# One-hot tables of the edge-MLP pass: four comparisons with a scalar per partition in place of one with two broadcast inputs

## The chip, the core and the metric

The kernel runs on one core of one Trainium2 chip. The metric is the device time of one execution in microseconds (us). Engines are named as in the profile: PE is TensorE, PEld its weight loads, DVE is VectorE, ACT is ScalarE, POOL is GpSimd, SP is SyncE. "TensorE clock" is the clock that the throttle granted, as a share of full speed.

## The reference

A graph network of four layers over 3125 nodes of 128 features and 100,000 edges that are sorted by destination. Each layer adds its result to the residual stream. The layer that this case touches is the second, a message pass with an MLP on every edge:

```
h = relu(layernorm(x))
x1   = concat(h[src], h[dst], edge_attr)          # 128 + 128 + 64 features
msgs = gelu(gelu(x1 @ mW1 + mb1) @ mW2 + mb2) @ mW3 + mb3
agg  = segment_sum(msgs, dst) / count
u    = gelu(concat(h, agg) @ uW1 + ub1) @ uW2 + ub2
x    = x + layernorm(u + h) * gamma + beta
```

The other layers are a GAT of three rounds (first), a GATv2 of two rounds with four heads (third), and a GCN of two rounds (fourth).

## The kernel before, in words

The edges are sorted into blocks of 128 destination nodes (25 blocks) and padded, so that a group of 512 edges has destinations in one block only. There are `NG` = 220 groups; a group is 4 tiles of 128 edges (`TG` = 4), with one edge per partition and the tile number along the free axis. `c.dlo[p, g, q]` holds, as an fp32 number, the destination of the edge at partition p, tile q, group g, counted from its block's first node. `c.iota` is a row 0 to 127 on every partition.

`mlp_pass` (line 1301) handles the 220 groups in a software pipeline of eight stages (`pipeline`, line 103): in one step each engine works on up to four groups at different stages. Loops run over `RING` = 8 steps, so buffers of eight (`rows`, `feat`, `hot`, `idxb`) are addressed by the step in the loop body. In one step:

- POOL runs ahead on its own: `gather_rows` (line 981) issues four indirect DMAs per group (line 989), one per tile, each of which takes 128 row numbers from `idxb` and fetches 128 rows of `source_table` into `rows`. It waits for the row numbers (ACT, line 1004) and for the use of `rows` eight groups earlier (`sum1`).
- PE: `add_up` (line 1395) multiplies the transposed one-hot tile `hot` with the messages `g2` into `ps_acc`; `second` (1404) is the second MLP layer; `first` (1414 to 1420) sums the destination part, the edge features and the gathered rows (it waits for the DMAs of `rows`); `turn` (1015, 1432) spreads the destinations and transposes the features of a later group.
- DVE, in this order: `featt` copied out of PSUM (1449), bias added to the second layer (`u2`, 1455), the edge weights written as a column of `g2` (1458, 4 elements per partition, SBUF to SBUF), the block's sum added to `c.acc` (1465), and last the one-hot table of a later group (1470, the helper `one_hot`, 1020 to 1028).
- ACT: the transposed one-hot `hott` (1486, 1490), two GELUs (1497, 1505), and the next row numbers (1004).
- SP: loads the edge features (1352) and stores `hot` and `hott` to DRAM (1359, 1363) for the GATv2 layer.

The order on each engine is the order in which the code is written; semaphores tie the engines together. PE uses a `hot` table five steps after DVE wrote it. `one_hot` has two forms: without a `weight` it is one `tensor_tensor` over 4 x 128 elements, with `iota` repeated over the tiles and `dlo` repeated over the 128 nodes; with a `weight` it is one `tensor_scalar` per tile, which compares `iota` with one number per partition and multiplies by `weight(k)`.

Of the kernel before, what the change touches and what calls it, by code (L numbers as in the profile page):

```python
# [42 lines left out]
RING = 8  # L43
# [49 lines left out]
def wait(eng, sem, value):  # L93

    if not isinstance(value, int) or value > 0:
        eng.wait_ge(sem, value)
# [6 lines left out]
def pipeline(nc, eng, depth, step, c=None, at=0):  # L103

    def blocks(g, n):
        if c is None:
            return [None] * n
        _, values = nc.values_load_multi_w_load_instructions(  # L110
            c.gblk[0:1, bass.ds(g, n)], engines=[eng.engine], min_val=0, max_val=NB - 1,
            skip_runtime_bounds_check_because="the sort counts the blocks that end before a group, NB - 1 at most")
        return values

    def plain(s, b):
        return [(*divmod(s + d, RING), b if d == at else None) if 0 <= s + d < NG else None for d in range(depth)]

    b = blocks(0, at + 1)
    for s in range(1 - depth, 1):
        step(plain(s, b[s + at] if s + at >= 0 else None))  # L120
    turns = (NG - depth) // RING
    with eng.Fori(0, turns) as i:
        b = blocks(RING * i + 1 + at, RING)
        for j in range(1, RING + 1):
            step([(*group_at(i, j + d), b[j - 1] if d == at else None) for d in range(depth)])
    last = RING * turns + 1
    b = blocks(last + at, NG - last - at)
    for s in range(last, NG):
        step(plain(s, b[s - last] if s + at < NG else None))
# [890 lines left out]
def one_hot(ve, c, out, g, weight=None):  # L1020

    if weight is None:
        return ve.tensor_tensor(out[:, :, :], c.iota[:, :].unsqueeze(1).to_broadcast([P, TG, BN]),
                                c.dlo[:, bass.ds(g, 1), :].rearrange("p a q -> p (a q)").unsqueeze(2)
                                .to_broadcast([P, TG, BN]), ALU.is_equal)
    for k in range(TG):
        ins = ve.tensor_scalar(out[:, k, :], c.iota[:, :], c.dlo[:, bass.ds(g, 1), k], weight(k), ALU.is_equal, ALU.mult)
    return ins
# [272 lines left out]
def mlp_pass(nc, c, table, recs, w1, b1, w2, b2, hots, hotts):  # L1301
# [3 lines left out]
    with ExitStack() as ctx:  # L1305
# [4 lines left out]
        hot = [sb(f"hot{r}", [P, TG, BN]) for r in range(RING)]  # L1310
# [16 lines left out]
        with phase(nc, "idx_ready", "in0", "in1", "in2", "in3", "in4", "in5", "in6", "in7", "feat0", "feat1", "feat2", "feat3", "feat4", "feat5", "feat6", "feat7", "w_in", "ones_set",  # L1327
# [9 lines left out]
            with nc.Block() as block:  # L1337
                @block.gpsimd
                def _(g):
                    gather_rows(g, table, rows, idxb, idx_ready, rows_in, sum1, begun)  # L1340
# [95 lines left out]
                @block.vector  # L1436
                def _(ve):
                    for k in range(4):
                        ve.memset(g2[k][:, :, D:D + 1], 1.0).then_inc(ones_set, 1)
                    ve.wait_ge(w_in, 64)  # L1440

                    def step(stages):
                        added, _, seconds, _, _, _, turned, _ = stages
                        if turned:
                            i, r, _ = turned
                            g = RING * i + r
                            ve.wait_ge(featt_ready, g + 1)
                            wait(ve, sum1, g - 3)
                            ve.tensor_copy(featt[r % 4][:, :], ps_featt[0:EF, :]).then_inc(featt_out, 1)  # L1449
                        if seconds:  # L1450
                            i, r, _ = seconds
                            g = RING * i + r
                            ve.wait_ge(sum2, g + 1)
                            wait(ve, gelu2, g)
                            ve.tensor_tensor(u2[:, :, :], ps_2[r % 2][:, :, :], b2r[:, :, :].to_broadcast([P, TG, D]), ALU.add) \
                                .then_inc(biased, 1)
                            wait(ve, agg_done, g - 3)
                            ve.tensor_scalar(g2[r % 4][:, :, D + 1], c.wgt[:, bass.ds(g, 1), :], 1.0, None, ALU.mult) \
                                .then_inc(wcol, 1)
                        if added:  # L1460
                            i, r, b = added
                            g = RING * i + r
                            ve.wait_ge(agg_done, g + 1)
                            wait(ve, acc_done, g)
                            ve.tensor_tensor(c.acc[:, bass.ds(b, 1), 0:MA], c.acc[:, bass.ds(b, 1), 0:MA],
                                             ps_acc[r % 2][:, 0:MA].unsqueeze(1), ALU.add).then_inc(acc_done, 1)
                        if turned:
                            i, r, _ = turned
                            wait(ve, hot_stored[r], 16 * i)
                            one_hot(ve, c, hot[r], RING * i + r).then_inc(hot_ready, 1)  # L1470
                    pipeline(nc, ve, 8, step, c, 0)

                @block.scalar
# [668 lines left out]
```

## Time and profile before

| | |
|---|---|
| median of 3 runs | 7726.31 us (7721.85 to 7735.73) |
| the profiled execution's own time | 7744.64 us |
| its span, first to last instruction | 7742.9 us |
| mean granted TensorE clock | 0.906 |
| PE / PEld busy over the span | 66% / 56% |
| DVE busy | 65% |
| ACT busy | 35% |
| POOL busy | 48% |
| the stage of `mlp_pass`, by the gathers' first and last start | 3259.9 to 4470.1 us |
| the gathers of that stage (line 989, `source_table`) | 880, 1072 ns mean |

The busy shares are means over stages that differ; what a change in `mlp_pass` is worth has to be read from the stretch between 3260 and about 4520 us. A row of a timeline gives the start, the duration, the engine, line and operation, the tiles, and in brackets the idle time before it. Its DVE durations overlap: an instruction starts before the tail of the one ahead is over.

### The profile page before, as it was taken

Reading aid. Unit: us, or ns where it says so; the run is one execution under the profiler, and the core shown is the slowest. Engines: PE = TensorE matmul, PEld = TensorE weight load, DVE = VectorE, ACT = ScalarE, POOL = GpSimd, SP = SyncE. Lnnn points to the kernel's source line nnn. Section 1 sums busy time; section 2 is a strip of 40 time slices with the busy share of each in tenths; the row PEclk is TensorE's granted clock in tenths of the full one; section 3 lists DMA queues with packets and bytes.
Section 4 is the critical chain, followed back from the end, with each engine's and each line's share of the span. In section 5 each row is a group of like instructions: output and inputs, shape, how many; then the busy total and the mean of one; then the engine's idle time right before and its main releaser. Section 6 shows DMA issues by size and latency. Waiting matters only on the chain. (4 is left out here: it accounts for less than half of the span.)

```text
span 7742.9 us, 154089 instructions
## 1 busy us (share of the span) xinstructions
PE 5149.0 (66%) x44603; PEld 4306.5 (56%) x44935; DVE 5031.7 (65%) x12351; ACT 2732.9 (35%) x6113; POOL 3754.8 (48%) x3623
## 2 busy tenths in 40 slices
PE   2111117666577768599988843888885688888477
PEld 1100102665466767466666633777774577777377
DVE  8554543999776868433333345888886698888521
ACT  1000000478664757244444431333332233333200
POOL 2777771234300000177777705777773477777100
PEclk9999999987799989799999976999997799999688
DMA  4111114234332424144555622444555344546355
GB/s 180 53 52 52 53 49 159 70 119 134 109 142 89 153 95 153 51 144 142 145 142 140 127 27 62 129 131 132 132 131 59 98 132 132 130 133 123 56 196 213
DMA packets 662773, 884.55 MB, mean 114 GB/s; under 512 B 304425, under 2 KB 487254, under 8 KB 643668
## 3 DMA queue, kind: packets, MB, share of 16 engines
q1 hardware_dynamic: 553028, 674.48, 26.8%
q0 software_dynamic: 109568, 207.74, 13.7%
q8 instruction: 108, 1.77, 0.1%
q14 instruction: 69, 0.57, 0.0%
HBM read 648.77 MB, written 233.08 MB: 114 GB/s over the span
## 5 line engine op out<-in xcount | busy, mean ns | idle before, releaser
L989 POOL DMA_INDIRECT rows<-head_table,idxb x1760 | 1709.9, 972 | 808.1 <-issue 462.3
L989 POOL DMA_INDIRECT rows<-source_table,idxb x880 | 943.2, 1072 | 1424.6 <-ACT idxb L1009 1156.7
L1707 DVE TENSOR_REDUCE gtop<-ps_top 128x1 f32<-128x512 f32 x1760 | 1204.2, 684 | 72.3 <-PE ps_top L1844 65.6
L363 POOL DMA_INDIRECT records<-recb,idxb x784 | 760.7, 970 | 257.3 <-issue 246.9
L787 PE MATMUL ps_cells<-hot 128*128 128x128 bf16 x4608 | 481.3, 248 | 257.0 <-DVE hot L745 109.1
L1449 DVE COPY featt<-ps_featt 64x512 f32<-64x512 f32 x220 | 150.2, 683 | 769.3 <-PE ps_featt L1432 762.5
L391 PE MATMUL ps_g<-hott 64*128 64x128 bf16 x784 | 59.6, 304 | 841.8 <-ACT hott L405 834.3
L1096 PE MATMUL ps_acc<-rows,pt 128*128 128x128 f32 x3750 | 515.4, 279 | 136.0 <-DVE pt L1117 120.6
L1844 PE MATMUL ps_top<-srow,sel 128*128 128x128 bf16 x7040 | 584.3, 230 | 10.1 <-DVE gtop L1707 3.0
L1096 PEld LDWEIGHTS ps_acc<-rows,pt 128*128 128x128 f32 x3750 | 460.4, 192 | 170.1 <-DVE pt L1117 162.3
L1856 PE MATMUL ps_acc<-val,hot 128*128 128x132 f32 x3520 | 539.4, 301 | 9.9 <-DVE val L1670 9.2
L787 PEld LDWEIGHTS ps_cells<-hot 128*128 128x128 bf16 x4608 | 356.6, 112 | 300.4 <-issue 281.7
L1844 PEld LDWEIGHTS ps_top<-srow,sel 128*128 128x128 bf16 x7040 | 485.1, 104 | 58.5 <-DVE gtop L1707 34.3
L391 PEld LDWEIGHTS ps_g<-hott 64*128 64x128 bf16 x784 | 33.7, 127 | 867.6 <-ACT hott L405 859.6
L729 POOL TENSOR_TENSOR none<-logs,far 128x640 f32<-128x640 f32 x125 | 256.4, 2051 | 498.9 <-ACT logs L819 498.9
L1765 ACT ACTIVATE parts<-sc 128x20 bf16<-128x20 f32 x444 | 97.2, 219 | 1101.0 <-DVE sc L1694 1029.2
L1856 PEld LDWEIGHTS ps_acc<-val,hot 128*128 128x128 f32 x3520 | 476.8, 208 | 12.9 <-DVE val L1670 10.5
L1819 PE MATMUL ps_sc<-att,bent 128*128 128x4 f32 x3520 | 462.3, 255 | 2.7 <-ACT bent L1782 2.5
L1819 PEld LDWEIGHTS ps_sc<-att,bent 128*128 128x128 f32 x3520 | 436.1, 195 | 17.0 <-ACT bent L1782 4.1
L745 DVE TENSOR_TENSOR hot<-hot,pair 128x2048 bf16<-128x2048 bf16 x282 | 404.2, 1486 | 13.4
L1670 DVE TENSOR_TENSOR val<-rows,p 128x528 f32<-128x528 f32 x440 | 309.5, 703 | 128.8 <-issue 128.8
L1830 PE MATMUL ps_e<-hott,mine 128*128 128x512 bf16 x1100 | 318.9, 388 | 100.7 <-DMA hot<-one_hots 84.0
(327 smaller groups left out, 12262.7 us busy)
## 6 DMA issues: line engine op xcount, KB each, us to landing
logs<-log_counts SPq DMA_DIRECT2D x75, 1600.0 KB
hot<-one_hots SPq DMA_DIRECT2D x440, 256.0 KB
wt<-edge_weights SPq DMA_DIRECT2D x50, 1600.0 KB
one_hots<-hot SPq DMA_DIRECT2D x220, 256.0 KB, 2.0
hott<-one_hots_t SPq DMA_DIRECT2D x440, 128.0 KB
edge_weights<-both SPq DMA_DIRECT2D x125, 320.0 KB, 2.8
log_counts<-none SPq DMA_DIRECT2D x125, 320.0 KB, 2.2
records<-blank SPq DMA_DIRECT2D x16, 1870.0 KB
```

Source lines behind the costliest of these rows:

```text
L363: g.indirect_dma_start(out=recs[:, :], out_offset=bass.IndirectOffsetOnAxis(ap=idxb[k][:, t:t + 1], axis=0), in_=recb[k][:, t, :], in_offs ...
L729: g.tensor_tensor(none[r][:, :, :], logs[r][:, :, :], far[r][:, :, :], ALU.subtract).then_inc(masked[r], 1)
L745: ins = ve.tensor_tensor(hot[k][:, m, :, :, :], hot[k][:, 1, :, :, :], value, ALU.mult)
L787: pe.matmul(tile[:, 0:P], hot[k][:, 0, j // 2, :, j % 2], hot[k][:, m, j // 2, :, j % 2], start=False, stop=m == 4, skip_group_check=True)
L989: g.indirect_dma_start(out=rows[r][:, k, :], out_offset=None, in_=table, in_offset=bass.IndirectOffsetOnAxis(ap=idxb[r][:, k:k + 1], axis= ...
L1096: ins = pe.matmul(ps_acc[b % 2][:, 0:D], pt[n % 4][:, t, :], c.rows[:, at, 0:D], start=at == 0, stop=at == NB - 1)
L1670: ve.tensor_tensor(val[k][:, :, :, :], rows[r][:, :, 0:HEADS * HW].rearrange("p q (f h) -> p q f h", h=HEADS), p[k][:, 0:SC].rearrange("p ...
L1707: ve.tensor_reduce(gtop[:, h:h + 1], ps_top[h % TOPS][:, :], AX.X, ALU.max).then_inc(topped, 1)
L1819: ins = pe.matmul(ps_sc[:, q * HEADS:(q + 1) * HEADS], bent[sr % 2][:, q * P:(q + 1) * P], att4[:, :], start=True, stop=True)
L1830: pe.matmul(ps_e[:, :], c.mine[:, bass.ds(b, 1), m, :].rearrange("p a f -> p (a f)"), hott[r][:, :], start=m == 0, stop=False)
L1844: ins = pe.matmul(ps_top[h % TOPS][:, q * P:(q + 1) * P], c.sel[:, q * HEADS + h, :], srow[:, :], start=True, stop=True)
L1856: ins = pe.matmul(ps_acc[:, 0:HEADS * HW], hot[r][:, q, :], val[k][:, q, :, :].rearrange("p f h -> p (f h)"), start=q == 0, stop=q == TG - 1)
```

## The change

In `mlp_pass`, DVE's call of `one_hot` gets a weight of 1.0, so that the helper takes its second form:

```diff
@@ mlp_pass, VectorE, step() @@
                         if turned:
                             i, r, _ = turned
                             wait(ve, hot_stored[r], 16 * i)
-                            one_hot(ve, c, hot[r], RING * i + r).then_inc(hot_ready, 1)
+                            one_hot(ve, c, hot[r], RING * i + r, lambda k: 1.0).then_inc(hot_ready, 1)
```

The helper, which is the same in both kernels:

```python
def one_hot(ve, c, out, g, weight=None):
    if weight is None:
        return ve.tensor_tensor(out[:, :, :], c.iota[:, :].unsqueeze(1).to_broadcast([P, TG, BN]),
                                c.dlo[:, bass.ds(g, 1), :].rearrange("p a q -> p (a q)").unsqueeze(2)
                                .to_broadcast([P, TG, BN]), ALU.is_equal)
    for k in range(TG):
        ins = ve.tensor_scalar(out[:, k, :], c.iota[:, :], c.dlo[:, bass.ds(g, 1), k], weight(k), ALU.is_equal, ALU.mult)
    return ins
```

The values in `hot` are the same. The program's order is the same on POOL, ACT, PE and SP. On DVE, inside the loop of `mlp_pass` (one of its eight steps), `hot` with its number is the one-hot buffer of the step, `iota` and `dlo` the inputs; ISA rows set up an address that depends on the loop counter:

```order
-L1023 ISA
-L1023 TENSOR_TENSOR hot_14515<-iota,dlo 128x512
+L1027 ISA
+L1027 TENSOR_SCALAR hot_14515<-iota,dlo 128x128
+L1027 ISA
+L1027 TENSOR_SCALAR hot_14515<-iota,dlo 128x128
+L1027 ISA
+L1027 TENSOR_SCALAR hot_14515<-iota,dlo 128x128
+L1027 ISA
+L1027 TENSOR_SCALAR hot_14515<-iota,dlo 128x128
```

One instruction of 512 elements per partition with two SBUF inputs became four of 128 elements with one SBUF input and one number per partition. They stand where it stood, at the end of the step behind lines 1458 and 1465, and the semaphore `hot_ready` is raised by the fourth.

## Rows read from the trace of the kernel before

**Rows 1.** Windows of the stage: busy us of each engine, PEclk, DMA share, GB/s.
```profile
3255.00:3460.00 205.00, 180.76 (x1132) 128.34 (x1151) 75.68 (x171) 95.33 (x186) 155.57 (x147) 0.91 0.52 148
...
3660.00:3860.00 200.00, 183.75 (x1193) 133.84 (x1209) 79.56 (x185) 96.31 (x185) 155.38 (x147) 0.95 0.51 144
...
4471.00:4525.00 54.00, 30.79 (x187) 23.33 (x188) 16.57 (x38) 13.35 (x27) 0.03 (x1) 0.82 0.62 72
```
**Rows 2.** Waits in 3300 to 4500 us: who waited for whom, us, times, longest.
```profile
POOL rows L989 <- issue: 250.5, 822, 0.3
PEld ps L1420 <- DMA rows<-source_table,idxb: 154.7, 95, 4.4
...
PE ps_acc L1395 <- DVE acc L1465: 31.9, 17, 2.3
...
POOL rows L989 <- ACT idxb L1004: 7.3, 24, 0.3
...
POOL rows L989 <- PE ps L1420: 1.2, 4, 0.3
```
**Rows 3.** Groups of instructions, 3255 to 4525 us: busy, mean ns, idle before.
```profile
L989 POOL DMA_INDIRECT rows<-source_table,idxb x880 | 943.2, 1072 | 1424.6 <-ACT idxb L1009 1156.7 <-issue 259.4 <-ACT idxb L1004 7.3
```
**Rows 4.** Groups of instructions by shape, DVE, 3300 to 4500 us.
```profile
L1449 DVE COPY featt<-ps_featt 64x512 f32<-64x512 f32 x211 | 144.1, 683 | 734.0 <-PE ps_featt L1432 727.2 <-PE ps L1420 4.0 <-issue 2.8
L1023 DVE TENSOR_TENSOR hot<-iota,dlo 128x512 f32<-128x512 f32 x211 | 142.8, 677 | 0.0
```
**Rows 5.** Durations of single instructions of lines 989 and 1458: min/median/max ns.
```profile
L989 POOL DMA_INDIRECT rows<-source_table,idxb x880: 940/946/1958, 3259.9 to 4470.1; - x176
L1458 DVE TENSOR_SCALAR g<-wgt x220: 151/154/372, 3279.9 to 4517.2; 128x4 f32 x104, 128x4 f32<-128x4 f32 x6
```
**Rows 6.** Timeline, POOL and DVE, one step from 3801.27 us: a long gather.
```profile
3801.27 1.86 POOL L989 DMA_INDIRECT rows<-source_table,idxb  x1 [0.30 <-issue]
3801.36 0.15 DVE L1458 TENSOR_SCALAR g<-wgt 128x4 f32 x1
...
3801.63 0.68 DVE L1023 TENSOR_TENSOR hot<-iota,dlo 128x512 f32<-128x512 f32 x1
...
3803.43 0.94 POOL L989 DMA_INDIRECT rows<-source_table,idxb  x1 [0.30 <-issue]
```
**Rows 7.** Timeline, POOL and DVE, from 3307.37 us: a short gather.
```profile
3307.37 0.95 POOL L989 DMA_INDIRECT rows<-source_table,idxb  x1 [0.31 <-issue]
3307.53 0.15 DVE L1458 TENSOR_SCALAR g<-wgt 128x4 f32 x1
...
3307.80 0.68 DVE L1023 TENSOR_TENSOR hot<-iota,dlo 128x512 f32<-128x512 f32 x1
```
**Rows 8.** Timeline, POOL and DVE, from 3302.23 us: a long line 1458.
```profile
3302.23 0.94 POOL L989 DMA_INDIRECT rows<-source_table,idxb  x1 [0.30 <-issue]
...
3302.80 0.37 DVE L1458 TENSOR_SCALAR g<-wgt 128x4 f32 x1
```
**Rows 9.** Timeline, POOL and DVE, in the GATv2 stage, from 4909.74 us.
```profile
4909.85 1.41 POOL L989 DMA_INDIRECT rows<-head_table,idxb  x1 [0.30 <-issue]
...
4909.74 0.70 DVE L1670 TENSOR_TENSOR val<-rows,p 128x528 f32<-128x528 f32 x1
4910.36 0.29 DVE L1675 TENSOR_TENSOR faded<-acc,p 128x132 f32<-128x132 f32 x1
```
**Rows 10.** Timeline of DVE from 1267.73 us: comparisons with a number per partition.
```profile
1267.73 5.63 DVE L659 TENSOR_SCALAR pick<-column,mine 128x512 f32<-128x512 f32 x14 [0.97 <-POOL mine L648]
```
**Rows 11.** Durations of single comparisons of that kind, two lines: min/median/max ns.
```profile
L659 DVE TENSOR_SCALAR pick<-column,mine x21: 477/479/485, 1267.7 to 1298.1; 128x512 f32<-128x512 f32 x21
L549 DVE TENSOR_SCALAR past<-at,first x25: 1000/1007/1079, 1169.1 to 1255.5; 25x1536 bf16<-25x1536 f32 x25
```
**Rows 12.** Timeline of PE: two steps that follow each other without a wait.
```profile
3818.01 0.65 PE L1420 MATMUL ps<-ident,rows 128*128 128x128 f32 x4
...
3822.75 0.66 PE L1420 MATMUL ps<-ident,rows 128*128 128x128 f32 x4
```

## The prediction

> **What bounds the kernel now.** The whole kernel has no single bound, so I read the stage that the change touches. In the windows of the stage PE is busy for 181 to 184 us of 200, DVE for 76 to 80, and POOL for 155.5, the same figure in every window [rows 1]. That looks like a stage bound by PE. The list of waits says otherwise: POOL never waits for anyone. Its idle time is 250.5 us in 822 pieces of 0.3 us, the fixed step from one indirect DMA to the next, and 8.5 us for ACT and PE together, while PE waits for the gathered rows (154.7 us on the side of its weight loads) [rows 2]. The sum closes: POOL's gathers begin at 3259.9 us, and 943.2 us busy + 259.4 + 7.3 + 1.2 = 1211.1 us of idle and busy time lead to the end of the last one at 4471 [rows 2, 3, 5]. So the stage lasts as long as POOL needs to issue 880 gathers, 1211/220 = 5.50 us for a group of four, and then some 50 us of drain.
>
> A gather has a length of its own: median 946 ns, minimum 940, but mean 1072 and maximum 1958 [rows 3, 5]. So 880 x (1.072 - 0.946) = 111 us of the stage are gathers that took longer than they need, 0.50 us per group. The timeline shows who makes them long. A gather that began at 3801.27 took 1.86 us; DVE began line 1458 at 3801.36 and the comparison of line 1023 at 3801.63, which ended at 3802.31, and the gather ended 0.82 us after that, at 3803.13 [rows 6]. In the GATv2 stage it is the same: the product of line 1670 ends at 4910.44 and the gather at 4911.26, 0.82 us later; line 1675, which follows it at once and also has two SBUF inputs, did not hold the gather a second time [rows 9]. So near its start a gather needs something that DVE holds while it runs an instruction with two inputs in SBUF; it then needs 0.82 us more. A gather that gets past this point is not held by the same comparison later on: at 3307.37 it took 0.95 us although line 1023 ran from 3307.80 [rows 7]. The opposite direction is there as well: line 1458, one input in SBUF and the output in SBUF, mostly takes 154 ns, but 0.37 us where it fell into the last part of a gather, and it ended when the gather did (3303.17) [rows 5, 8]. So an instruction of line 1458's kind collides with the gather's second half, and one of line 1023's kind only with its beginning.
>
> **The change part by part.** Removed per group: one comparison of 677 ns [rows 4]. Added: four of 128 elements. Their price comes from comparisons of the same kind. 14 of them with 512 elements ran in 5.63 us, each 0.479 long, so (5.63 - 0.479)/13 = 0.396 us apart; from 512 to 1536 elements the duration grows by (1007 - 479)/1024 = 0.52 ns per element [rows 10, 11]. For 384 elements less that is 0.198 less: 0.281 us long and 0.198 apart. Four are 3 x 0.198 + 0.281 = 0.875 us, 0.20 more than before. (If one ran at one element per cycle, as line 1023 does, it would be some 0.07 longer and the four 1.14 us; the slope speaks against it.)
>
> On DVE itself these 0.20 us, 44 us over 220 groups, cost nothing: DVE idles 734/211 = 3.48 us per step ahead of line 1449, and the comparisons are the last of the step [rows 4]. Four address computations instead of one go under the same cover, as does the later `hot_ready`: SP stores `hot` then, and PE uses it five steps on. PE's 17 waits for DVE's line 1465, 31.9 us, are the only place where DVE is late for PE [rows 2]; should all of them grow by 0.2 us it is 3.4 us, and PE has that much slack against POOL. Without cover the price would be the 44 us.
>
> What counts is POOL, three terms.
>
> (1) A gather held by the present comparison. A full stall is 1.86 - 0.95 = 0.91 us, so the 111 us are about 122 full stalls. The gather of rows 6 would be let in when the first of the new comparisons ends, 0.27 + 0.281 = 0.55 us behind the start of line 1458 instead of 0.95, 0.40 earlier, if DVE gives way between two instructions, as it did between lines 1670 and 1675 [rows 9]. But in rows 6 the gather was not let in when line 1458 ended at 3801.51 either, though the comparison began 0.12 us later: DVE's next instruction is in line well before it starts. With one more comparison in line the gain is 0.20. I take the middle, 0.30: 122 x 0.30 = 37 us saved.
>
> (2) A gather whose second half falls into the comparisons. Today it costs nothing [rows 7]. The new ones are of line 1458's kind, which collides there [rows 8]. The comparisons fill 0.875 us of the 1.25 from gather to gather, so in about 0.7 of the groups one begins its second half in them; it waits for half a spacing, 0.10 us: 220 x 0.7 x 0.10 = 15 us added.
>
> (3) Comparisons that wait for a gather: up to 0.37 us each, on DVE, under the cover above: 0.
>
> Sum: -37 + 15 = -22 us. The stage stays bound by POOL: even without any stall a group needs 5.50 - 0.50 = 5.00 us of it, and PE, where it waits for nothing, steps in 4.74 us (3818.01 to 3822.75) [rows 12]. Against the profiled execution's 7744.6 us this is 7723; the median of the runs lies 18 us lower, so 7726.3 - 22 = 7704.
>
> The trace of before has no run of four such comparisons beside gathers, so the bounds: from below, all stalls vanish, -111 us (7615). From above, DVE keeps what it holds from the first to the fourth: every stall ends 0.20 later, at most one per group, +44; and a gather caught in its second half waits for the rest of the chain, half of 0.875 = 0.44 us in 0.7 x 220 groups, half of which were held at their beginning anyway, +34. Together +78 (7804). I take a value nearer to the middle, because rows 9 show a hand-over between two instructions.
>
> **Rivals.**
>
> *Slower: the four act as one longer block.* Mechanism: the next comparison is in line before the last has ended, so the gather gets no turn between them, as it got none between lines 1458 and 1023 in rows 6. Price: 122 x 0.20 = 24 for the stalls of today, 34 for the second halves: +58, 7784. It decides as soon as gathers are released only by the fourth comparison. For it: rows 6. Against it: rows 9. The Trainium skill, in "SBUF — State Buffer" (Who interferes with whom), speaks for this side: it says that a `tensor_tensor` with two SBUF inputs contends only with GpSimd's reads, and that descriptor generation, which writes, should escape it, while a `tensor_scalar` in its two-port mode locks GpSimd out for the whole instruction. By that rule the change would put a stall where none was, and the side would be this rival's, 7784 or above. The trace agrees with the second half (line 1458 and gathers exclude each other) but not with the first: the comparison of rows 6 held the gather for 0.91 us.
>
> *No difference: the terms cancel.* Savings of 0.20 per stall, 24 us, against 15 to 25 for second halves; 7726. For it: only an instruction or two in line are needed. Against: nothing in the rows fixes either number.
>
> *Much faster: a gather gets its turn at once.* The spacing of 0.198 us with a read of a number per partition in front of each comparison leaves gaps, and the gather slips into the first of them. Then most of the 111 us go, and what remains is 15 us of short waits and a fifth of the stalls: about -70, 7656. For it: the comparisons of rows 10 follow each other less closely than their rate of 0.52 ns per element would allow (0.396 against 0.267). Against: rows 6.
>
> **How the numbers follow.** A measurement of this kernel tells about 0.2%, 15 us, from no change. Forecast (let in behind the first or second comparison): 0.36; one block: 0.27; cancelling: 0.20; at once: 0.17. The forecast's own range is -40 to -5 us, 7686 to 7721, and about two thirds of it is beyond 15 us. Faster: 0.36 x 0.7 + 0.17 + a little of the cancelling case = 0.45; slower 0.29; same 0.26. The range reaches from the third rival's 7656 to the first's 7784, rounded to 7650 and 7785; what lies outside is the rest of the two bounds.
>
> **What the profile after would show.** Four comparisons of about 0.28 us, 0.20 apart, on line 1027 (880 in place of 220); the mean of the stage's gathers at (1072 - 22/0.88 =) 1047 ns, with the median still at 946; the last gather starting near 4448 us. Long gathers should end about 0.82 us after the first or second comparison's end, and some comparisons should be stretched by up to 0.37 us by a gather's second half. If long gathers end 0.82 after the fourth, the block rival is right, and their mean is above 1.1 us. If the mean stays at 1.07 while the time falls, POOL did not bound the stage. If PE's waits for line 1465 grow beyond 50 us, DVE's cover was not there. If the comparisons take 0.35 us each, they do not run at the rate of rows 11. The other stages should not move.

## The result

The changed kernel takes 7629.8 us (median of 4 runs, 7627.2 to 7637.7) against 7731.0 for the kernel before (4 runs). By the medians it is 101 us faster; the ratio is 0.9872, interval [0.9855, 0.9889]. The forecast was 7704, its range ended at 7650, so the time lies outside it, beyond the rival called "at once" (7656) and close to the bound from below (7615), to which I had given next to nothing.

The profile of the changed kernel (span 7626.8 us) shows where the time went. First the groups of instructions between 3255 and 4425 us; the columns are as in [rows 3]:

```profile
L989 POOL DMA_INDIRECT rows<-source_table,idxb x880 | 834.4, 948 | 1426.5 <-ACT idxb L1009 1158.6 <-issue 256.6 <-PE ps L1420 9.1
```

The 880 gathers were busy for 943.2 us [rows 3] and are now for 834.4, 108.8 less. Their single durations, and those of the comparisons and of line 1458 (min/median/max ns), answer to [rows 5]:

```profile
L989 POOL DMA_INDIRECT rows<-source_table,idxb x880: 940/944/1141, 3259.9 to 4361.2; - x176
...
L1027 DVE TENSOR_SCALAR hot<-iota,dlo x880: 263/273/493, 3261.8 to 4407.5; 128x128 f32<-128x128 f32 x176
...
L1458 DVE TENSOR_SCALAR g<-wgt x220: 152/154/399, 3281.1 to 4417.7; 128x4 f32 x104, 128x4 f32<-128x4 f32 x6
```

The median of a gather is what it was; the tail is gone: 1141 ns at most, where it was 1958. The last gather starts at 4361.2 instead of 4470.1 us, 108.9 us earlier, and this is the gain of the whole kernel within the scatter of single executions (101 us by the medians, 116 between the two profiled ones). The waits of 3300 to 4400 us, as in [rows 2]:

```profile
POOL rows L989 <- issue: 247.2, 811, 0.3
...
PEld ps L1420 <- DMA rows<-source_table,idxb: 51.0, 38, 4.3
...
PE ps_acc L1395 <- DVE acc L1465: 23.0, 12, 2.1
...
POOL rows L989 <- PE ps L1420: 9.1, 30, 0.3
...
POOL rows L989 <- ACT idxb L1004: 2.1, 7, 0.3
```

POOL still has no idle piece longer than its own 0.3 us step, and the weight loads of PE wait a third as long for the rows (51.0 against 154.7 us). One window of each engine, as in [rows 1]:

```profile
3660.00:3860.00 200.00, 191.22 (x1321) 136.63 (x1321) 94.33 (x320) 103.93 (x200) 151.46 (x160) 1.00 0.58 158
```

160 gathers in 200 us are 40 groups, 5.00 us each: the floor that the prediction worked out for POOL without any stall. DVE is busier (94 against 80 us), at no cost. PE is now busy for 191 of these 200 us.

The timeline shows the case of [rows 6] under the new comparisons. Line 1458 again starts 0.08 us behind the gather, and the gather takes 0.94 us instead of 1.86:

```profile
4342.51 0.94 POOL L989 DMA_INDIRECT rows<-source_table,idxb  x1 [0.30 <-issue]
...
4342.59 0.15 DVE L1458 TENSOR_SCALAR g<-wgt 128x4 f32 x1
4342.66 0.28 DVE L1465 TENSOR_TENSOR acc<-acc,ps_acc 128x130 f32 x1
4342.86 0.86 DVE L1027 TENSOR_SCALAR hot<-iota,dlo 128x128 f32<-128x128 f32 x4
```

Where a gather's second half and the comparisons do meet, it is DVE that waits. Here the gather keeps its 0.94 us and the four comparisons take 1.01 instead of 0.86:

```profile
3752.45 0.94 POOL L989 DMA_INDIRECT rows<-source_table,idxb  x1 [0.30 <-issue]
...
3752.43 1.01 DVE L1027 TENSOR_SCALAR hot<-iota,dlo 128x128 f32<-128x128 f32 x4
```

Counted off the timelines of the stage: before, 158 of the 880 gathers took 1.0 us or more, 82 of them 1.7 to 1.96 us; after, 42 took 1.0 to 1.14 and none more. Of the 158, 156 ended 0.82 us (within 0.04) after the end of a comparison.

One other reading has to be met: the new comparisons might only have moved DVE and POOL against each other, so that fewer gathers meet them. The two traces say that this is at most the smaller part. Within 0.45 us of the start of a step's first comparison, 174 gathers began before and 158 after; the mean excess over 0.944 us is 0.63 us for the first and 0.01 us for the second. If each gather of the changed kernel is given the mean stall that gathers of its position had in the kernel before, 89 of the 112 us of stalls would be left (an estimate); 4 are.

### The profile page after: what moved, and what is told of

The parts are those of the page before. It is cut to its first block and busy times, and to the rows that moved or that the text cites. A ratio compares the mean times of both kernels' runs of the same rounds, so it can differ in the third digit from the quotient of the medians.

```text
span 7626.8 us, 155704 instructions
## 1 busy us (share of the span) xinstructions
PE 5123.1 (67%) x44934; PEld 4263.9 (56%) x44935; DVE 5081.9 (67%) x13011; ACT 2730.4 (36%) x6113; POOL 3644.1 (48%) x3623
## 5 line engine op out<-in xcount | busy, mean ns | idle before, releaser
L989 POOL DMA_INDIRECT rows<-source_table,idxb x880 | 834.4, 948 | 1426.5 <-ACT idxb L1009 1158.6
L1830 PE MATMUL ps_e<-hott,mine 128*128 128x512 bf16 x1320 | 365.4, 386 | 87.8 <-DMA hot<-one_hots 87.7
```

What stands on the lines that cost most here:

```text
L989: g.indirect_dma_start(out=rows[r][:, k, :], out_offset=None, in_=table, in_offset=bass.IndirectOffsetOnAxis(ap=idxb[r][:, k:k + 1], axis= ...
L1830: pe.matmul(ps_e[:, :], c.mine[:, bass.ds(b, 1), m, :].rearrange("p a f -> p (a f)"), hott[r][:, :], start=m == 0, stop=False)
```

## The experiments

Four questions: is it the comparison's second input in SBUF, its length, or its place behind line 1465 that held the gathers; and does the stage follow the gathers alone? The table has every kernel that was run where the kernel before takes about 7730 us, ordered by the mean of its 880 gathers. The time is the median of all executions, the mean gather is from the one that was profiled. The last column is 7632 + 880 x (mean - 0.950), the changed kernel's time in the second group plus the longer gathers. The changed kernel of the result (0.948, 7629.8) and of this table are the same.

| kernel | mean gather, us | time, us | ratio to before | by the gathers |
|---|---|---|---|---|
| f2_psum | 0.945 | 7629.5 | 0.9869 [0.9852, 0.9885] | 7628 |
| a1 (changed) | 0.950 | 7632.3 | 0.9868 [0.9851, 0.9884] | 7632 |
| f1_tt4 | 0.960 | 7641.2 | 0.9880 [0.9864, 0.9897] | 7641 |
| e4_after_psum | 0.961 | 7648.8 | 0.9888 [0.9872, 0.9905] | 7642 |
| e8_before_wait | 0.972 | 7657.8 | 0.9898 [0.9882, 0.9915] | 7651 |
| e9_tt2 | 0.978 | 7653.3 | 0.9896 [0.9879, 0.9912] | 7657 |
| f5_after_ts880 | 1.049 | 7722.2 | 0.9986 [0.9977, 0.9996] | 7719 |
| before | 1.063, 1.072 | 7726 to 7738 (profiled: 7726, 7745) | 1 | 7731, 7739 |

The median time follows the mean gather to within 7 us in every row. Since POOL has no longer waits in these kernels either, this shows that the gathers set the length of this stage.

### First group: one part of the difference at a time

The code cuts of this section are shortened; `repeated` and the like stand for the access patterns of the helper. Four comparisons, but of the old kind, with two inputs in SBUF:

```diff
-one_hot(ve, c, hot[r], RING * i + r).then_inc(hot_ready, 1)
+for q in range(TG):
+    ins = ve.tensor_tensor(hot[r][:, q:q + 1, :], iota_repeated, dlo_of_tile_q_repeated, ALU.is_equal)
+ins.then_inc(hot_ready, 1)
```

> From the kernel before: the one comparison of 512 elements with two SBUF inputs becomes four of 128 elements of the same kind, also with two SBUF inputs. Theory S (what holds a gather is a second SBUF input on VectorE, from the moment the instruction is in line): the four follow each other without a gap, the gather gets no turn, the gathers of source_table stay at 1.07 us mean or longer and the time at 7726 or up to 60 more. Theory L (what counts is how long one instruction holds; a gather gets its turn between two instructions): each holds for 0.3 us at most, mean of the gathers 0.95 to 0.98, time 7630 to 7660.

One comparison of the old length with one input from PSUM (in 214 of the 220 steps; the first six keep the old comparison, and `acc_done` is raised a little later than before):

```diff
+ve.tensor_copy(ps_acc[k][:, 384:512], c.iota[:, :])        # both banks, once
-one_hot(ve, c, hot[r], RING * i + r).then_inc(hot_ready, 1)
+ve.tensor_tensor(hot[r], ps_acc[added[1] % 2][:, 384:512] repeated, dlo repeated, ALU.is_equal)
+    .then_inc(hot_ready, 1)                                # then acc_done is raised
```

> From the kernel before: still one comparison of 512 elements, but the row of node numbers is read from PSUM (spare columns of the ps_acc bank that the step has just read), so that one input is in SBUF and the instruction is as long as before (0.68 us). The semaphore for the bank is raised behind the comparison instead of behind line 1465. Theory S: with a single SBUF input it holds no gather, mean 0.945 us, time about 7630, as with the change. Theory L: one long instruction still holds, mean 1.07, time 7726.

The changed kernel and, ahead of the four, a spare instruction: the old comparison (e3), or one long `tensor_scalar` with one SBUF input (e5):

```diff
+one_hot(ve, c, spare, RING * i + r)                                   # e3
+ve.tensor_scalar(spare[:, :], c.dlo (880 numbers), 1.0, None, ALU.mult)   # e5
 one_hot(ve, c, hot[r], RING * i + r, lambda k: 1.0).then_inc(hot_ready, 1)
```

> From the changed kernel: ahead of the four comparisons the old one is done as well (512 elements, two SBUF inputs), into a spare tile that nobody reads. Theories S and L both: the hold is back, mean of the gathers 1.05 to 1.10 us, time 7715 to 7745. If the gain came from something else that the four comparisons do to the order of the work, the time stays near 7630, since VectorE has 2.9 us idle in a step.

> From the changed kernel: ahead of the four comparisons one long tensor_scalar of 880 fp32 elements, SBUF to a spare tile in SBUF that nobody reads, with one SBUF input, in the mode of two elements per cycle (about 0.6 us, nearly as long as the old comparison). Theory S: no second input, so the gathers stay at 0.945 to 0.96 us and the time at 7630 to 7640. Theory L: a long instruction that shares something with the gather's writing half holds it for up to 0.6 us, mean 1.02 to 1.06, time 7690 to 7730.

This group gave no times to go by. It ran on another chip, where the kernel before takes 8982.5 us, not 7731, and the four were within 0.4% of it, none faster (ratios 1.0030, 1.0035, 1.0021, 1.0008). The granted TensorE clock of its executions is 0.85 to 0.86 against 0.90 to 0.92 in all others, and the stage is longer: 1532 us from the first gather to the last in e1 against 1210 in the kernel before. The waits of e5 between 3500 and 4900 us say why the stage does not follow the gathers there:

```profile
POOL rows L989 <- ACT idxb L1004: 308.0, 76, 7.4
...
PEld ps L1421 <- issue: 172.3, 213, 1.5
...
POOL rows L989 <- PE ps L1421: 44.7, 10, 4.8
```

POOL waits for the others, up to 7.4 us, and all engines have longer idle pieces that nothing in the profile explains (1.5 us in the second row). What is different about that chip stays open. The gathers' own durations can still be read: means of 0.962 (e1), 0.944 (e2), 1.017 (e3) and 1.005 us (e5). e3 shows that the old comparison brings the holds back beside the four new ones, though less than expected (1.05 to 1.10). Theory S, that only a second SBUF input holds a gather, fell with e1 (four such instructions hold little) and e5 (one without it holds much). The other half of S stands with e2: a long instruction with one input in PSUM holds none. Theory L had 1.07 there, so it failed in e2. The one long hold of e2 (1.44 us) belongs to one of the first six comparisons, which still read both inputs from SBUF; it ended 0.82 us after that comparison.

### Second group: anchors, the control, and "in line"

> The changed kernel again, as the anchor of this group of runs. In the first group the kernel before took 8982 us, against 7731 in the runs of the result: VectorE, ScalarE and TensorE stood idle for other reasons there, and GpSimd waited for row numbers (361 us) and for TensorE (62 us), so that the gathers did not set the length of the stage. If the stage is bound by the gathers (about 7730 before), the ratio is again 0.987; where it is not (about 8980 before), the shorter gathers buy nothing, ratio 0.997 to 1.003. In either case the mean of the gathers is 0.945 to 0.955 us.

> The kernel before again, for a profile from the same chip as its neighbours. Where the stage is bound by the gathers: POOL waits for nothing, mean of the gathers 1.07 us. Where it is not: POOL waits for row numbers, the mean of the gathers is lower, 1.02 to 1.05 us, since fewer of them meet a comparison.

The kernel before is at 7738.4 us (median of 7), its profiled execution at 7726.2 with a mean gather of 1.063; the changed kernel at 7632.3 with 0.950. The result repeats.

The control is the changed kernel with a spare comparison of 512 elements, its node numbers from PSUM (as in e2, into a tile nobody reads; `acc_done` is raised behind the comparisons, later than in the changed kernel):

> From the changed kernel: ahead of the four comparisons one more of 512 elements into a spare tile, with the node numbers from PSUM, so one input in SBUF; as long as the old one (0.68 us). It is the control for the two spare instructions of the first group, which brought the mean of the gathers to 1.017 us (two inputs in SBUF, 0.677 us) and 1.005 us (one input and output in SBUF at two elements per cycle, 0.607 us). Theory P (a hold needs the second port pair of SBUF, which an instruction takes for a second SBUF input or for two elements per cycle): mean stays at 0.945 to 0.955. Theory D (any long VectorE instruction there delays the gathers, or the time shift does): mean about 1.01.

0.961 us, 11 ns over the changed kernel and 6 above the end of the expected range, where the spare instructions of e3 and e5 had brought 1.017 and 1.005. So it is neither the longer step nor any long instruction, and theory P stands in the main. What is left is not from the spare one: none of the 48 gathers that began 0.05 to 0.45 us ahead of it took over 0.948 us, and of the 99 that took 1.0 us or more, 38 began in the first 0.2 us of the four comparisons behind it. Why these hold more here than in the changed kernel is open. The median of 7648.8 us is 16 above the changed kernel, 10 of them by the gathers; the profiled execution, from which the gathers are, took 7641.5.

Then the old comparison, kept from being in line early:

```diff
+if added:
+    ve.wait_ge(acc_done, RING * added[0] + added[1] + 1)   # line 1465 is over
 one_hot(ve, c, hot[r], RING * i + r).then_inc(hot_ready, 1)
```

> From the kernel before: the old comparison waits until line 1465 is over, so it can't be in line while lines 1458 and 1465 run. Theory Q (the comparison holds the gather from the moment it is in line, some 0.3 us before its own start): the stretch in which a gather is caught shrinks from about 0.95 to 0.68 us, so the mean of the gathers falls from 1.072 to 1.00 to 1.03 us, and the time by 35 to 65 us where the gathers bound the stage; no gather that began more than 0.1 us ahead of the comparison is held. Theory R (line 1458 holds the gather itself and hands over to the comparison): mean and time as before.

An added wait made the kernel 81 us faster than the one before by the medians (7657.8 against 7738.4). The gathers' mean is 0.972 and no stall is longer than 0.52 us (1.464 - 0.94). Of the next two gathers, the first starts 0.33 us ahead of the comparison and is free; the second starts 0.08 us behind the comparison's start and is held to its end and 0.83 us more:

```profile
3301.83 0.95 POOL L989 DMA_INDIRECT rows<-source_table,idxb  x1 [0.30 <-issue]
...
3616.69 1.44 POOL L989 DMA_INDIRECT rows<-source_table,idxb  x1 [0.30 <-ACT idxb L1004]
```

```profile
3302.16 0.69 DVE L1023 TENSOR_TENSOR hot<-iota,dlo 128x512 f32<-128x512 f32 x1 [0.21 <-DVE acc L1465]
...
3616.61 0.69 DVE L1023 TENSOR_TENSOR hot<-iota,dlo 128x512 f32<-128x512 f32 x1 [0.23 <-DVE acc L1465]
```

Of the gathers that began 0.05 to 0.45 us ahead of the comparison, 111 of 135 took over 1.2 us in the kernel before, and none of 112 here (one took 1.18). So theory Q holds, with a larger effect than it had put down (1.00 to 1.03, 35 to 65 us): the comparison held gathers from the time it stood in line behind lines 1458 and 1465, not from its own start. Theory R, that line 1458 itself holds the gather, fails: of the gathers that began within 0.15 us of line 1458's start, 72 of 75 took over 1.2 us before, and none of 58 took over 0.96 us here. The case of [rows 7], a free gather in that position, belongs to the other 24, most of which began over 0.40 us ahead of the comparison; that one began 0.43 ahead, the gather of [rows 6] 0.36.

### Third group: the same parts where the gathers bound the stage

> The same kernel as e1_tt4 (four comparisons of 128 elements with two SBUF inputs each), in the hope of a group of runs in which the gathers bound the stage. Theory T (VectorE holds the gather with one instruction at a time, its own length and what it stands in line, and the gather gets its turn before the next): mean of the gathers 0.960 us as in e1_tt4, so (0.960 - 0.948) x 880 = 11 us slower than the changed kernel: 7640 to 7650, ratio to before 0.988 to 0.990. Theory I (the kind matters, two inputs hold across the four): 1.05 or more, 7710 to 7740.

> The same kernel as e2_psum (one comparison of 512 elements, the node numbers from PSUM). Mean of the gathers 0.944 us, as in e2_psum: 880 x (0.948 - 0.944) = 3 us faster than the changed kernel, 7620 to 7635, ratio 0.985 to 0.988. If the length of the one instruction counted on its own: 7726, ratio 1.0.

Both came out as theory T said (7641.2, 7629.5). f2_psum, one instruction and no hold at all, is level with the changed kernel: the intervals of their ratios in the table are almost the same. Only 4 of its gathers took 1.0 us or more, all in the first 26 us of the stage, while the first comparisons still read both inputs from SBUF. The gathers of f2_psum, then the gathers and comparisons of f1_tt4:

```profile
L989 POOL DMA_INDIRECT rows<-source_table,idxb x880 | 831.5, 945 | 1425.2 <-ACT idxb L1009 1157.2 <-issue 253.3 <-PE ps L1420 10.4
```

```profile
L989 POOL DMA_INDIRECT rows<-source_table,idxb x880 | 844.7, 960 | 1425.3 <-ACT idxb L1009 1157.4 <-issue 259.7 <-PE ps L1420 7.0
...
L1471 DVE TENSOR_TENSOR hot<-iota,dlo 128x128 f32<-128x128 f32 x880 | 195.2, 278 | 0.0
```

In f1_tt4 the four comparisons take the same DVE time as those of the change (195 us against 193) and have two SBUF inputs each. The step from the old kernel to them, splitting alone, is 7733.7 - 7641.2 = 92 of the 101 to 106 us. The other kind of instruction adds some 9 us by the mean gather (0.960 against 0.950); the two times are from different groups, and the intervals of their ratios overlap.

> The same kernel as e5_after_ts880 (changed kernel with one spare tensor_scalar of 880 elements ahead of the four, 0.607 us, one input in SBUF). In the first group it held gathers up to 1.90 us, mean 1.005. Theory T: a hold by length whatever the kind, so where the gathers bound the stage, mean 1.01 to 1.06 and time (1.01 to 1.06 - 0.948) x 880 = 55 to 100 us above the changed kernel, 7685 to 7730. Theory K (only a second input holds): mean 0.95, 7630.

7722.2 us and 1.049: one spare instruction of 0.61 us with one SBUF input gives nearly the whole gain back. On its timeline it also holds gathers at a place where the old comparison did not, about their middle: of the gathers that began 0.46 to 0.60 us ahead of it, 46 of 50 took 1.0 us or more; at that distance from the old comparison none of 27 did. The gather below starts 0.50 us before it and ends 0.52 us after its end:

```profile
3529.19 1.62 POOL L989 DMA_INDIRECT rows<-source_table,idxb  x1 [0.30 <-issue]
```

```profile
3529.69 0.60 DVE L1472 TENSOR_SCALAR spare<-dlo 128x880 f32<-128x880 f32 x1
```

> From the kernel before: two comparisons of 256 elements with two SBUF inputs, each about 0.41 us. It is the middle dose between one of 0.677 us (mean of the gathers 1.063 to 1.072) and four of 0.276 (0.962 in e1_tt4). Theory T: the stall a gather meets goes with about the square of the length of one hold, times their number: mean about 0.99 to 1.02, time 7665 to 7695. Theory I: as before, 7726 or above.

The middle dose is not in the middle: two of 256 elements already bring 80 of the 101 us (0.978 us, 7653.3), below the range that I had written. As many gathers are held as in the kernel before (172 of 1.0 us or more, against 158), each for 0.17 us on average in place of 0.71. So halving the instruction takes away more than half of the stall: its length counts more than in proportion.

## Why the prediction was wrong

**Right: the bound and the place.** POOL's gathers set the stage's length, and the comparison held them. Table and result show both. The floor of 5.00 us per group was met, the DVE terms were right (four in 0.86 us, worked out as 0.875; hidden), and nothing in the waits shows a cost of the later `hot_ready`. The other stages hardly moved: the last gather of this stage came 109 us earlier, and the two profiled executions differ by 116.

**Wrong: term (1), the 0.30 us saved per stall.** The prediction took the gather of [rows 6] and let it wait for the first or second of the new comparisons, because "DVE's next instruction is in line well before it starts". The observation was right, and e8 shows it. What was wrong is the step from there: that the new comparison in line would hold the gather in the same way. It did not: in the changed kernel none of the 73 gathers that began 0.05 to 0.45 us ahead of the first comparison took over 1.004 us. Measured, term (1) was 109 us, not 37 (112 us of stalls over 0.944 us a gather before, 4 after). f1_tt4 puts most of this on the split: with two inputs each, the stalls still fall from 112 us in sum to 14.

Within this the size of a stall also worked against me. I divided 111 us by the longest kind, 0.91 us, and got 122. There were 158, of 0.71 us on average. A sum of stalls says nothing about their lengths; the durations in the timeline would have.

**Wrong: term (2), 15 us for second halves.** The comparisons do collide with them: their mean is 286 ns against a median of 273, their maximum 493. But the gather was there first, and the comparison waited; it cost some 12 us (880 x 0.013) of DVE's idle time, while the gathers lost 4 us in all. The prediction charged to POOL what term (3) had already charged to DVE. It would have been right for a long instruction, as f5_after_ts880 shows.

**The rivals.** "One longer block" (0.27) rested on rows 6; e1, f1 and e9 say that a gather gets its turn between two instructions that follow each other, as between lines 1670 and 1675 in [rows 9]. That was the better evidence, since it had two such instructions in a row and rows 6 had only one. "At once" (0.17) had the right outcome and was priced too low, with a fifth of the stalls left; 3 to 5% were. Its reason, gaps that come from reading a number per partition, is not shown: the comparisons of f1_tt4 read none, and seven eighths of the stalls go there too.

**The rule that the slower rival leaned on.** By the Trainium skill, "SBUF — State Buffer" (Who interferes with whom), a `tensor_scalar` in its two-port mode locks GpSimd out, and a `tensor_tensor` with two SBUF inputs contends with GpSimd's reads but, as the page infers, not with descriptor generation. f5_after_ts880 bears out the first (mean gather 1.049 us). The inference is contradicted by the kernel before, e8 and e9 (1.072, 0.972 and 0.978): that kind holds the start of an indirect DMA. Whether it does so through the DMA's own read of its row numbers from `idxb` in SBUF, which the rule on reads would allow, no run here separates. The same section's statement that the first to issue keeps the pair fits what the comparisons met, which waited for gathers that had begun (493 ns at most in place of 273).

**Open.** Why a second instruction in line lets the gather through. In f1_tt4 a gather that met the first comparison was mostly released at the end of the second (13 of the 17 that began in its first 0.1 us). The one below starts 0.08 us behind the first comparison and ends at 3538.98; 0.82 us before that, at 3538.16, the second comparison ends (3537.68 + 0.48; the row has the two).

```profile
3537.76 1.22 POOL L989 DMA_INDIRECT rows<-source_table,idxb  x1 [0.30 <-issue]
```

```profile
3537.68 0.48 DVE L1471 TENSOR_TENSOR hot<-iota,dlo 128x128 f32<-128x128 f32 x2
```

Some 13 others, which had begun ahead of it, were released as the first began (their end is 0.82 us after its start). No run here separates the rule behind the two. Why the four comparisons with a number per partition hold even less than those of f1_tt4 (4 us against 14) is open as well.

## What to carry to other kernels

An engine that never waits for anyone and has instructions with a mean well above their median (here 1072 against 946 ns) may be the bound of its stage even at 78% busy; look up in the timeline what runs on the other engines while the long ones do. While GpSimd issues indirect DMAs, give VectorE short instructions, or one input in PSUM, rather than one long instruction that works on SBUF alone: four of 0.28 us in place of one of 0.68 made VectorE busy for 44 us more (193 against 149), out of its idle time, and saved 101. A price that is read from one kind of collision, one instruction with nothing behind it, does not carry over to a sequence of short ones.

## What the runs showed that I had not expected

- A wait added on an engine with time to spare made the kernel 81 us faster (e8_before_wait): it kept an instruction from standing in line.
- Splitting one 0.677 us instruction into two of 0.410 took three quarters of the stalls away (112 us to 30), into four of 0.278 seven eighths (to 14).
- One spare 0.61 us `tensor_scalar` per step, where VectorE had 2.8 us of idle time in a step, cost 90 us (7632.3 to 7722.2).
- In one group of runs the kernel before took 8982.5 us instead of about 7730, and in all four kernels of that group POOL waited for row numbers in the stage (308 us in e5). There the shorter gathers bought nothing.
